# The attention phase of a two-layer network: next rows turned and projected half a slot sooner, their norms' root moved around one mask, and the layernorm chain in three pieces

## The chip, the core and the metric

The kernel runs on one core of one Trainium2 chip. The metric is the device time in microseconds (us). The program has six phases, one after the other, and the change touches the third alone, the linear attention.

Five engines run their own queues in program order and meet at semaphores: TensorE (PE, with its weight loads as PEld), VectorE (DVE), ScalarE (ACT), GpSimd (POOL) and the queues that issue transfers (SP and POOL).

## The reference

Two transformer layers of width 256 on 4 batches of 1024 rows. The attention of the second layer is linear, with positive random features. Cut to what matters here:

```python
qkv = x @ Wqkv + bqkv                                   # 4 x 1024 rows, 16 heads of 16
xn = x / jnp.maximum(jnp.linalg.norm(x, axis=-1, keepdims=True), 1e-12)      # q and k, per head
proj = jnp.einsum('bhtd,rhdm->rbhtm', xn, omega)
feat = jnp.exp(jnp.clip(proj * sqrt_2s - s, -20.0, 20.0)) / np.sqrt(M) ...   # 64 features
# in chunks of 128 rows, with a state carried from chunk to chunk:
kv_cur = jnp.cumsum(kv_prod, axis=2) + kv_state
ctx = jnp.einsum('bhtf,bhtfd->bhtd', q_ch, kv_cur)
out = (ctx / den) @ Wout + bout
x = _layernorm(x + out)
```

## The kernel before, in words

`phase_attention` walks the 1024 rows in eight steps of 128 rows (for all four batches), and each step has eight slots, one for each pair of heads. `body(i)` of every engine writes step i, with the slots t = 0 to 7; bodies -1 and 8 lead in and out. The order on each engine is fixed by this text.

The work of a pair is spread over three slots. In slot t, PE computes the features of pair t (L1192, six matmuls), the scores and turned keys of pair t-1 (L1204, L1210) and the context of pair t-2 (L1224, L1229, L1235). DVE clips the features of pair t (L1380), masks the scores of pair t-1 (L1385) and adds to the state for pair t-2 (L1391). ACT takes the exponentials of pair t (L1270, two), copies the keys of pair t-1 (L1275) and the context of pair t-2 (L1279).

The features have one place in PSUM: PE's features of the next pair wait for DVE's clip of this one. The scores of a pair wait for the mask of the pair before.

Between these stand the projections. A table, `SLOTS_OF_X`, names them by slot and by one of three points: A (after the features), B (after the scores and keys) and C (after the context). The names are: FT, rows of the next step turned; FQ, their q and k projected (FQ 0 to 3, one for each batch); FV, v of this step; FN, normed q and k of the next step turned; BO, context of the step before turned; BC, its quotient turned; BW, its output projection. Each is some matmuls on PE (L1151, L1131, L1162, L1168, L1171) into one of two PSUM banks in turn, and a read by DVE in the same place of its order (`x_evac`); FT, FN and BC are first copied by ACT (`x_high`). A step may start on PE once the step two before it in this order has been read.

Four chains run beside them:

- The norms of the next step's q and k: POOL squares the rows of two batches at a time (L1100) when FQ 1 and FQ 3 have been read; DVE sums (`squares`, L1399), and finds 1/sqrt by a guess (`norm_guess`, L1404 to L1406) and three Newton steps (`norm_newton`, L1409 to L1411), each operation waiting for the one before; POOL multiplies (L1105, in two halves), and PE's FN 0 waits for the first half.
- The layernorm of the step before: DVE's `row_stats` (L1423) when BW has been read, `row_moments` and `row_scales` (L1427 to L1437, the root in L84 to L89), and ACT's `normalise` (L1294).
- The output of BW is written to `z`, which waits until `normalise` of the step before has read it.
- In steps 1 to 6 the weights of the experts are split for a later phase, four chunks a step: ACT rounds a chunk (`expert_high`, L1287, slots 1 to 4), POOL subtracts (L1083), issues a store and a load (L1085, L1087). On POOL, chunks 0 to 2 stand ahead of the two squarings, chunk 3 behind the two multiplications.

Of the kernel before, what the change touches and what calls it, by code (L numbers as in the profile page):

```python
# [9 lines left out]
I32 = mybir.dt.int32  # L10
ALU = mybir.AluOpType
# [4 lines left out]
BATCH, SEQ, D = 4, 1024, 256  # L16
# [63 lines left out]
def rsqrt(chain, v, r, t, ti, ready=None):  # L80


    ve = chain.eng
    chain.link(ve.tensor_scalar(ti, v.bitcast(I32), 1, None, ALU.logical_shift_right))  # L84
    chain.link(ve.tensor_scalar(r.bitcast(I32), ti, -1.0, float(0x5F3759DF), ALU.mult, ALU.add))  # L85
    for n in range(3):
        chain.link(ve.scalar_tensor_tensor(t, r, -0.5, r, ALU.mult, ALU.mult))  # L87
        chain.link(ve.tensor_tensor(t, t, v, ALU.mult))  # L88
        ins = ve.scalar_tensor_tensor(r, t, 1.5, r, ALU.add, ALU.mult)  # L89
        if n == 2 and ready is not None:  # L90
            ins.then_inc(ready, 1)
        else:
            chain.link(ins)
# [810 lines left out]
def phase_attention(nc, x2, bqkv, bout, masks, x3, routed_w, wlo, ids, rows_out, x2_stored, x3_stored, early, x0, x0_in, fc):  # L904

    with ExitStack() as ctx:
# [3 lines left out]
        def sem(name):  # L910
# [52 lines left out]
        A_, B_, C_ = range(3)  # L963
        SLOTS_OF_X = {0: ((B_, "FN", 3), (C_, "BO", 2)),
                      1: ((A_, "BC", 0), (C_, "FV", 0), (C_, "FV", 1)),
                      2: ((A_, "BO", 3), (B_, "FT", 0), (C_, "FT", 1)),
                      3: ((A_, "BC", 1), (B_, "FQ", 0), (C_, "FQ", 1)),
                      4: ((A_, "BW", 0), (B_, "FQ", 2), (C_, "FQ", 3)),
                      5: ((A_, "BW", 1), (C_, "BO", 0)),
                      6: ((A_, "BO", 1), (C_, "FN", 0)),  # L970
                      7: ((A_, "FN", 2), (C_, "FN", 1))}
# [3 lines left out]
        def is_step(n):  # L975
            return not isinstance(n, int) or 0 <= n < STEPS
# [277 lines left out]
        @block.scalar  # L1254
        def _(act):
            act.activation(fc[:, LNA], fc[:, QBIAS], ACT.Ln).then_inc(s["ln_done"], 1)

            def x_high(i, t, point):
                for _, _, name, a, n, h in x_at(i, t, point):
                    if name in HI:  # L1260
                        act.wait_ge(s["x_done"], n + 1)
                        dst = {"FT": xts, "FN": qkt, "BC": ctxt}[name][:, 0, a, :]
                        act.activation(dst, ps[:, x_bank(i, name, a), :], ACT.Copy).then_inc(s["x_hi"], 1)

            def exponentials(n, u):
                act.wait_ge(s["clip_done"], n + 1)

                wait(act, "pair_done", n - 3)
                for q, (dst, bias) in enumerate(((qf, QBIAS), (kf, KBIAS))):
                    act.activation(dst[:, u % 4, :], cf[:, u % 2, q], ACT.Exp, bias=fc[:, bias]).then_inc(s["exp_done"], 1)  # L1270

            def key_rows(n, u):
                act.wait_ge(s["kt_done"], n + 1)
                wait(act, "pair_done", n - 1)
                act.activation(kr[:, u % 2].rearrange("p b f -> p (b f)"), ps[:, KT, :], ACT.Copy).then_inc(s["kr_ready"], 1)  # L1275

            def context_out(i, n, u):
                act.wait_ge(s["pair_done"], n + 1)
                act.activation(ot[:, u], ps[:, OB, 0:2 * P], ACT.Copy).then_inc(s["ot_ready"], 1)  # L1279

            def expert_high(i, c):

                n = (i - 1) * EPER + c
                k = c % 2
                act.wait_ge(eraw_in[k], 16 * ((i - 1) * EPER // 2 + c // 2 + 1))
                act.wait_ge(elo_ready, PRIMED + n)
                act.activation(ehi[:], eraw[:, k], ACT.Copy).then_inc(ehi_ready, 1)  # L1287

            def normalise(i):
                act.wait_ge(s["stats_ready"], i)  # L1290
                act.wait_ge(x2_stored, PRIMED + 16 * STEPS)
                act.wait_ge(s["stored"], PRIMED + 16 * (i - 1))
                for b in range(BATCH):
                    last = act.activation(out[:, b, :], z[:, b, :], ACT.Identity, bias=small[:, 5, b:b + 1], scale=small[:, 3, b:b + 1])  # L1294
                last.then_inc(s["out_ready"], 1)

            def body(i):
                for t in range(PAIRS):
                    if isinstance(i, int) and i == 0 and t == 0:
                        act.wait_ge(s["fc_ready"], 1)  # L1300
                    x_high(i, t, A_)
                    if pair(i, t, 0) is not None:
                        exponentials(*pair(i, t, 0))
                    if pair(i, t, 1) is not None:
                        key_rows(*pair(i, t, 1))
                    x_high(i, t, B_)
                    if pair(i, t, 2) is not None:
                        context_out(i, *pair(i, t, 2))
                    if t == 1 and is_step(i - 2):
                        normalise(i - 1)  # L1310
                    x_high(i, t, C_)
                    if 1 <= t <= EPER and (not isinstance(i, int) or 1 <= i < LAST):
                        expert_high(i, t - 1)
                if isinstance(i, int) and i == STEPS:
                    normalise(i)

            body(-1)
            body(0)
            body(1)
            with act.Fori(2, LAST) as i:  # L1320
                body(i)
            body(LAST)
            body(STEPS)

        @block.vector
        def _(ve):
# [69 lines left out]
            def squares(ch, f, half):  # L1396
                ve.wait_ge(s["sq_ready"], 2 * f + half + 1)
                per = BATCH * HEADS1
                ch.mark(ve.tensor_reduce(nv[:, half * per:(half + 1) * per],  # L1399
                                         sq[:, 2 * half:2 * half + 2].rearrange("p b (n d) -> p (b n) d", d=HD), AX.X, ALU.add))  # L1400
# [7 lines left out]
            def norm_newton(ch, last):  # L1408
                ch.link(ve.scalar_tensor_tensor(nt, nr, -0.5, nr, ALU.mult, ALU.mult))  # L1409
                ch.link(ve.tensor_tensor(nt, nt, nv, ALU.mult))  # L1410
                ins = ve.scalar_tensor_tensor(nr, nt, 1.5, nr, ALU.add, ALU.mult)  # L1411
                if last:
                    ins.then_inc(s["rnorm_ready"], 1)
                else:
                    ch.link(ins)
# [16 lines left out]
                ch.link(ve.tensor_scalar(v, v, 1.0 / D, EPS, ALU.mult, ALU.add))  # L1432
                ch.link(ve.scalar_tensor_tensor(v, half_, 0.25, v, ALU.mult, ALU.add))

            def row_scales(ch):
                rsqrt(ch, v, r, t_, smalli[:])
                ve.tensor_tensor(nb, mean, r, ALU.mult).then_inc(s["stats_ready"], 1)  # L1437
                ch.end()

            def body(i):  # L1440
                norm = Chain(ve, s["norm_own"], NORM_OWN)
                rows = Chain(ve, s["ln_own"], LN_OWN)
                front, back = is_step(i + 1), is_step(i - 1)
                if front:
                    norm.turn(i + 1)
                for t in range(PAIRS):
                    if pair(i, t, 0) is not None:
                        clip(*pair(i, t, 0))
                    x_evac(i, t, A_)
                    if front and t == 6:  # L1450
                        norm_newton(norm, False)
                    if isinstance(i, int) and i == 0 and t == 1:
                        ve.wait_ge(s["weights_in"], WEIGHTS)
                    if pair(i, t, 1) is not None:
                        mask(*pair(i, t, 1))
                    x_evac(i, t, B_)
                    if front and t == 4:
                        squares(norm, i + 1, 0)
                    if front and t == 5:
                        squares(norm, i + 1, 1)  # L1460
                    if front and t == 6:
                        norm_newton(norm, True)
                        norm.end()
                    if pair(i, t, 2) is not None:
                        new_state(*pair(i, t, 2))
                    x_evac(i, t, C_)
                    if front and t == 5:
                        norm_guess(norm)
                        norm_newton(norm, False)
                    if back and t == 6:  # L1470
                        rows.turn(i - 1)
                        row_stats(rows, i)
                    if t == 0 and is_step(i - 2):
                        rows.turn(i - 2)
                        rows.n = BATCH
                        row_moments(rows)
                        row_scales(rows)
                    if isinstance(i, int) and i == STEPS and t == 7:
                        row_moments(rows)
                        row_scales(rows)  # L1480

            body(-1)
            body(0)
# [924 lines left out]
```

## Time and profile before

| | |
|---|---|
| median of 3 runs | 1588.9 us (1588.62 to 1590.71) |
| the profiled execution | 1574.64 us, span 1573.1 us |
| PE busy in the span | 1399.0 us (89%) |
| DVE busy | 920.3 us (59%) |
| ACT busy | 688.8 us (44%) |
| POOL busy | 517.8 us (33%) |
| attention, from its first instruction to its last | about 323 to 848 us of the span |

Busy time is an average over six phases. The rows further down are all of the attention but for three on the clock. A slot is told from the start of its clip (L1380) to the start of the next.

### The profile page before, as it was taken

To read this page: it belongs to the slowest core of one execution; us is meant where nothing else is said; L and a number is where in the kernel's file an instruction comes from. 1 tells how busy PE (TensorE), PEld (TensorE's weight loads), DVE (VectorE), ACT (ScalarE), POOL (GpSimd) and SP (SyncE) were. 2 spreads that over 40 slices of the span, in tenths; PEclk is the share of its full clock that TensorE was granted. 3 is DMA by queue.
4 is the path that set the end of the run, shared out by engine and by line. 5 is a ranking of instruction groups with operands and counts; after the bars stand their busy time and mean duration, and the time that the engine had idled before them with its cause. 6 is when DMAs were issued, how large, how long until landed. Compare 5 with 4: busy or idle time off the path is not lost. (4 is left out here: it accounts for less than half of the span.)

```text
span 1573.1 us, 34052 instructions
## 1 busy us (share of the span) xinstructions
PE 1399.0 (89%) x12248; PEld 1208.8 (77%) x12248; DVE 920.3 (59%) x1994; ACT 688.8 (44%) x1260; POOL 517.8 (33%) x395
## 2 busy tenths in 40 slices
PE   6799999849889889889894899999979999999980
PEld 5688888737667667667673888888879999999980
DVE  4766666656667766777774336443435555555544
ACT  2457656513435435345343323222224555555543
POOL 0245544420343343244300002542203444444440
PEclk7799999959889999999996899999999999999995
DMA  6234321120123133132114601333228888888865
GB/s 250 87 122 149 134 95 63 54 82 15 46 91 110 51 107 123 50 120 93 40 29 152 253 27 61 136 106 116 95 82 224 231 235 242 235 237 230 235 161 220
DMA packets 101209, 204.07 MB, mean 130 GB/s; under 512 B 18448, under 2 KB 72720, under 8 KB 94864
## 3 DMA queue, kind: packets, MB, share of 16 engines
q1 hardware_dynamic: 76032, 144.73, 28.7%
q0 software_dynamic: 23088, 54.31, 12.1%
q10 hardware_dynamic: 2016, 4.08, 0.7%
q8 instruction: 44, 0.72, 0.2%
q14 instruction: 29, 0.24, 0.0%
HBM read 144.53 MB, written 58.55 MB: 129 GB/s over the span
## 5 line engine op out<-in xcount | busy, mean ns | idle before, releaser
L2132 PE MATMUL e_ps<-e_xhl,e_whl 128*128 128x256 f32 x1872 | 248.1, 282 | 5.1 <-DMA e_whl<-wlo 5.1
L2132 PEld LDWEIGHTS e_ps<-e_xhl,e_whl 128*128 128x128 f32 x1872 | 232.9, 189 | 5.6 <-issue 5.6
L1723 PE MATMUL d_ps<-d_xhl,d_whl 128*128 128x512 f32 x768 | 194.8, 403 | 5.3 <-DVE d_whl L1793 5.3
L1723 PEld LDWEIGHTS d_ps<-d_xhl,d_whl 128*128 128x128 f32 x768 | 145.1, 194 | 35.2 <-issue 5.6
L2028 POOL DMA_INDIRECT xs<-e_y,e_slot_id x78 | 121.5, 1558 | 82.8 <-ACT e_y L2059 68.1
L382 POOL TENSOR_TENSOR b_hhl<-b_h,b_hhl 128x512 fp32r<-128x512 f32 x64 | 94.4, 1477 | 138.5 <-ACT b_hhl L609 112.2
L2112 PE MATMUL e_ps<-e_whl,e_ghl 128*128 128x256 f32 x936 | 137.7, 282 | 0.5 <-DVE e_ghl L2206 0.5
L2194 DVE TENSOR_TENSOR e_g<-e_ps,e_act_h 128x256 f32<-128x256 f32 x156 | 66.2, 424 | 116.1 <-ACT e_act_h L2073 115.9
L2112 PEld LDWEIGHTS e_ps<-e_whl,e_ghl 128*128 128x128 f32 x936 | 120.5, 188 | 0.7 <-ACT e_ghl L2083 0.7
L1898 DVE TENSOR_TENSOR d_g<-d_ps,d_act_h 128x512 f32<-128x512 f32 x64 | 44.2, 691 | 127.6 <-PE d_ps L1723 93.9
L475 PE MATMUL b_ps<-b_w,b_hhl 128*128 128x256 f32 x768 | 105.5, 287 | 6.6 <-DVE b_turned_rows L702 5.6
L475 PEld LDWEIGHTS b_ps<-b_w,b_hhl 128*128 128x128 f32 x768 | 99.2, 193 | 12.8 <-issue 6.0
L2073 ACT ACTIVATE e_act_h<-e_ps 128x256 f32<-128x256 f32 x156 | 59.9, 384 | 111.3 <-PE e_ps L2132 111.3
L1270 ACT ACTIVATE c_qf<-c_cf,fc 128x512 f32<-128x512 f32 x64 | 46.3, 723 | 138.9 <-DVE c_cf L1380 138.9
L1702 PEld LDWEIGHTS d_ps<-d_whl,d_ghl 128*128 128x128 f32 x768 | 100.9, 191 | 4.8
L462 PE MATMUL b_ps<-b_xhl,b_w 128*128 128x512 f32 x384 | 104.1, 406 | 0.5 <-ACT b_h L606 0.5
L1702 PE MATMUL d_ps<-d_whl,d_ghl 128*128 128x256 f32 x768 | 104.2, 286 | 0.0
L1083 POOL TENSOR_TENSOR c_elo<-c_eraw,c_ehi 128x1024 fp32r<-128x1024 f32 x24 | 57.0, 2373 | 133.8 <-ACT c_ehi L1287 109.9
L2021 POOL CAST e_whl<-wall 128x1024 fp32r x39 | 40.5, 1039 | 166.1 <-PE e_ps L2112 118.6
L2206 DVE TENSOR_TENSOR e_ghl<-e_g,e_ghl 128x256 fp32r<-128x256 f32 x156 | 66.0, 423 | 41.3 <-ACT e_ghl L2083 41.1
L1380 DVE TENSOR_SCALAR c_cf<-c_ps,fc 128x1024 f32<-128x1024 f32 x64 | 85.7, 1338 | 6.0 <-PE c_ps L1192 4.6
L1769 ACT ACTIVATE d_ghl<-d_g 128x512 fp32r<-128x512 f32 x64 | 40.4, 632 | 103.5 <-DVE d_g L1898 101.3
(304 smaller groups left out, 2686.9 us busy)
## 6 DMA issues: line engine op xcount, KB each, us to landing
e_whl<-wlo SPq DMA_DIRECT2D x39, 1024.0 KB, 5.1
e_whl<-wlo SPq DMA_DIRECT2D x39, 512.0 KB, 3.7
c_eraw<-in_expert_w POOLq DMA_DIRECT2D x24, 512.0 KB, 4.8
wlo<-c_elo POOLq DMA_DIRECT2D x24, 512.0 KB, 3.0
wall<-in_expert_w SPq DMA_DIRECT2D x8, 1536.0 KB, 8.5
xg<-b_zeros POOLq DMA_DIRECT2D x13, 780.0 KB, 3.9
e_xr<-xg SPq DMA_DIRECT2D x39, 260.0 KB, 3.9
x<-rows_out SPq DMA_DIRECT2D x16, 512.0 KB, 3.1
```

The lines of the kernel that those rows point to most:

```text
L382: gp.tensor_tensor(hhl[:, m % 4, 1], h[:, m % 4], hhl[:, m % 4, 0].bitcast(F32), ALU.subtract).then_inc(s["hlo_ready"], 1)
L462: mm = pe.matmul(ps[:, H + m % 2, :], w1s[:, wp, kd, m * P:(m + 1) * P], xhl[:, k, xp, kd, :], start=q == 0, stop=q == 3 * KD - 1)
L475: mm = pe.matmul(ps[:, O + b // 2, lo:lo + D], hhl[:, m % 4, hp, b * P:(b + 1) * P], w2s[:, wp, m, :], start=m == 0 and q == 0 and b % 2 = ...
L1380: ve.tensor_scalar(cf[:, u % 2], ps[:, FB:FB + 2, :], fc[:, HIGH], fc[:, LOW], ALU.min, ALU.max).then_inc(s["clip_done"], 1)
L1702: mm = pe.matmul(ps[:, O + b // 2, (b % 2) * D:(b % 2 + 1) * D], ghl[:, m % 4, gp_, b * P:(b + 1) * P], whl[:, wp_, m // HM, lo:lo + D], s ...
L1723: mm = pe.matmul(ps[:, H + 2 * (m % 2) + w, :], whl[:, wp, e, lo:lo + P], xhl[:, k, xp, kd, :], start=q == 0, stop=q == 3 * KD - 1)
L2028: gp.indirect_dma_start(xs, bass.IndirectOffsetOnAxis(ap=slot_id[:, i, b:b + 1], axis=0), y[:, k, b, :], None, compute_op=ALU.add).then_in ...
L2073: act.activation(act_h[:, m], ps[:, H + m, 0:SLOT], ACT.Silu).then_inc(s["silu_done"], 1)
L2112: mm = pe.matmul(ps[:, O + k, b * D:(b + 1) * D], ghl[:, m, gp_, b * P:(b + 1) * P], whl[:, k, wp_, lo:lo + D], start=m == 0 and q == 0 an ...
L2132: mm = pe.matmul(ps[:, H + m, w * SLOT:(w + 1) * SLOT], whl[:, k, wp, lo:lo + P], xhl[:, k, xp, kd, :], start=q == 0, stop=q == 3 * KD - 1)
L2194: ve.tensor_tensor(g[:, m], ps[:, H + m, SLOT:2 * SLOT], act_h[:, m], ALU.mult).then_inc(s["g_ready"], 1)
L2206: ve.tensor_tensor(ghl[:, m, 1], g[:, m], ghl[:, m, 0].bitcast(F32), ALU.subtract).then_inc(s["glo_ready"], 1)
```

## The change

The table of steps, two lines of it (slots 0, 1 and 5 to 7 stay; in slots 2 to 4 the same steps stand at other points):

```diff
-                      2: ((A_, "BO", 3), (B_, "FT", 0), (C_, "FT", 1)),
-                      3: ((A_, "BC", 1), (B_, "FQ", 0), (C_, "FQ", 1)),
+                      2: ((A_, "FT", 0), (B_, "FT", 1), (C_, "BO", 3)),
+                      3: ((A_, "FQ", 0), (B_, "FQ", 1), (C_, "BC", 1)),
```

ACT's layernorm output goes from the middle of slot 1 to the end of slot 3:

```diff
-                    if t == 1 and is_step(i - 2):
+                    x_high(i, t, C_)
+                    if t == 3 and is_step(i - 2):
                         normalise(i - 1)
-                    x_high(i, t, C_)
```

DVE: the root of the norms is all in slot 5, and the layernorm's chain, which stood whole in slot 0, is now in slots 0, 1 and 3. Its first part, `row_stats`, goes from slot 6 to slot 7.

```diff
+            def row_chain(rows, i, t):
+
+                if t == 0:
+                    rows.turn(i - 2)
+                    rows.n = BATCH
+                    row_moments(rows)
+                if t == 1:
+                    row_guess(rows)
+                    row_newton(rows)
+                if t == 3:
+                    row_newton(rows)
+                    row_newton(rows)
+                    row_shift(rows)
...
                     x_evac(i, t, A_)
-                    if front and t == 6:
+                    if front and t == 5:
+                        squares(norm, i + 1, 1)
+                        norm_guess(norm)
                         norm_newton(norm, False)
...
                         mask(*pair(i, t, 1))
                     x_evac(i, t, B_)
+                    if pair(i, t, 2) is not None:
+                        new_state(*pair(i, t, 2))
+                    if front and t == 5:
+                        norm_newton(norm, False)
+                        norm_newton(norm, True)
+                        norm.end()
+                    x_evac(i, t, C_)
                     if front and t == 4:
                         squares(norm, i + 1, 0)
-                    if front and t == 5:
-                        squares(norm, i + 1, 1)
-                    if front and t == 6:
-                        norm_newton(norm, True)
-                        norm.end()
-                    if pair(i, t, 2) is not None:
-                        new_state(*pair(i, t, 2))
-                    x_evac(i, t, C_)
-                    if front and t == 5:
-                        norm_guess(norm)
-                        norm_newton(norm, False)
-                    if back and t == 6:
+                    if is_step(i - 2):
+                        row_chain(rows, i, t)
+                    if back and t == 7:
```

`row_guess`, `row_newton` and `row_shift` are the two, three and one instructions that `row_scales` held.

DVE's queue in slot 5, before: from the sums of the second two batches (L1399) to the clip of slot 6.

```order
L1399 TENSOR_REDUCE c_nrm<-c_sq 128x64
L1391 TENSOR_TENSOR c_state<-c_ps,c_state 128x128
L1360 TENSOR_SCALAR c_den<-c_ps 128x16
L1361 RECIPROCAL c_den<-c_den 128x16
L1363 TENSOR_TENSOR c_cr<-c_ps,c_den 128x2x4x32
L1404 TENSOR_SCALAR c_nrm<-c_nrm 128x128
L1405 TENSOR_SCALAR c_nrmi<-c_nrm 128x128
L1406 TENSOR_SCALAR c_nrm<-c_nrmi 128x128
L1409 SCALAR_TENSOR_TENSOR c_nrm<-c_nrm 128x128
L1410 TENSOR_TENSOR c_nrm<-c_nrm 128x128
L1411 SCALAR_TENSOR_TENSOR c_nrm<-c_nrm 128x128
L1380 TENSOR_SCALAR c_cf<-c_ps,fc 128x1024
```

DVE's queue in slot 5 of the changed kernel, from the same sums on; L1360, L1361, L1363 and the clip of slot 6 follow behind it.

```order
L1399 TENSOR_REDUCE c_nrm<-c_sq 128x64
L1404 TENSOR_SCALAR c_nrm<-c_nrm 128x128
L1405 TENSOR_SCALAR c_nrmi<-c_nrm 128x128
L1406 TENSOR_SCALAR c_nrm<-c_nrmi 128x128
L1409 SCALAR_TENSOR_TENSOR c_nrm<-c_nrm 128x128
L1410 TENSOR_TENSOR c_nrm<-c_nrm 128x128
L1411 SCALAR_TENSOR_TENSOR c_nrm<-c_nrm 128x128
L1385 TENSOR_TENSOR c_sm<-c_ps,c_tri 128x1024
L1391 TENSOR_TENSOR c_state<-c_ps,c_state 128x128
L1409 SCALAR_TENSOR_TENSOR c_nrm<-c_nrm 128x128
L1410 TENSOR_TENSOR c_nrm<-c_nrm 128x128
L1411 SCALAR_TENSOR_TENSOR c_nrm<-c_nrm 128x128
```

The sums, the guess and the first Newton step now stand ahead of slot 5's mask (L1385), which stood ahead of the sums, and the other two steps, which stood in slot 6 on both sides of its mask, come right behind it.

ACT's queue in slot 3 and at the start of slot 4, before: the quotient's copy (BC 1), the exponentials, the keys, the context copy, and chunk 2 of the experts (L1287).

```order
L1263 ACTIVATE c_ctxt<-c_ps 128x512
L1266 REGISTER_ALU
L1270 ACTIVATE c_qf<-c_cf,fc 128x512
L1270 ACTIVATE c_kf<-c_cf,fc 128x512
L1275 ACTIVATE c_kr<-c_ps 128x512
L1279 ACTIVATE c_ot<-c_ps 128x256
L1285 ISA
L1286 REGISTER_ALU
L1287 ACTIVATE c_ehi<-c_eraw 128x1024
L1266 REGISTER_ALU
L1270 ACTIVATE c_qf<-c_cf,fc 128x512
L1270 ACTIVATE c_kf<-c_cf,fc 128x512
```

The same place in the changed kernel, from slot 3's context copy on.

```order
L1279 ACTIVATE c_ot<-c_ps 128x256
L1261 REGISTER_ALU
L1263 ACTIVATE c_ctxt<-c_ps 128x512
L1292 ISA
L1294 ACTIVATE rows_out<-c_z,c_small 128x256 x4
L1285 ISA
L1286 REGISTER_ALU
L1287 ACTIVATE c_ehi<-c_eraw 128x1024
L1266 REGISTER_ALU
L1270 ACTIVATE c_qf<-c_cf,fc 128x512
L1270 ACTIVATE c_kf<-c_cf,fc 128x512
L1275 ACTIVATE c_kr<-c_ps 128x512
```

BC 1's copy now stands behind the context copy, and the layernorm's output (L1294) with its wait stands between it and chunk 2.

## Rows read from the trace of the kernel before

**Rows 1.** Waits, 330 to 850 us: engine, line, what for, us in total, times, longest.

```profile
PE c_ps L1162 <- POOL c_sq L1105: 46.4, 8, 10.5
```

**Rows 2.** Windows (length; PE, PEld, DVE, ACT, POOL busy; clock; DMA): slot 6, one step.

```profile
576.99:587.88 10.89, 5.73 (x67) 3.65 (x65) 7.01 (x18) 2.68 (x5) 5.69 (x3) 0.79 0.00 0
576.99:638.68 61.69, 56.39 (x714) 42.31 (x713) 44.55 (x89) 27.84 (x48) 23.86 (x17) 0.94 0.28 93
```

**Rows 3.** Timeline: start, duration, what, idle before and its releaser; slot 6.

```profile
582.19 3.82 POOL L1105 TENSOR_TENSOR c_sq<-c_qk,c_nrm 128x1024 f32<-128x1024 f32 x2 [10.95 <-DVE c_nrm L1411]
...
584.17 1.12 PE L1162 MATMUL c_ps<-ident,c_sq 128*128 128x128 f32 x4 [5.16 <-POOL c_sq L1105]
```

**Rows 4.** Timeline of PE: the features that open slots 0, 1, 2, 4, 5 and 6.

```profile
592.82 0.97 PE L1192 MATMUL c_ps<-c_qkt,early 32*128 32x512 f32 x6
...
598.15 0.97 PE L1192 MATMUL c_ps<-c_qkt,early 32*128 32x512 f32 x6
...
606.48 0.96 PE L1192 MATMUL c_ps<-c_qkt,early 32*128 32x512 f32 x6
...
620.29 0.96 PE L1192 MATMUL c_ps<-c_qkt,early 32*128 32x512 f32 x6
...
629.22 0.97 PE L1192 MATMUL c_ps<-c_qkt,early 32*128 32x512 f32 x6
...
635.74 0.50 PE L1192 MATMUL c_ps<-c_qkt,early 32*128 32x512 f32 x2
```

**Rows 5.** Timelines of ACT (slot 1), POOL and DVE (slot 4), same step.

```profile
606.24 2.07 ACT L1294 ACTIVATE rows_out<-c_z,c_small 128x256 f32<-128x256 f32 x4
608.20 1.05 ACT L1287 ACTIVATE c_ehi<-c_eraw 128x1024 fp32r<-128x1024 f32 x1
...
622.60 2.37 POOL L1083 TENSOR_TENSOR c_elo<-c_eraw,c_ehi 128x1024 fp32r<-128x1024 f32 x1 [1.88 <-DMA wlo<-c_elo]
...
626.79 1.91 POOL L1100 TENSOR_TENSOR c_sq<-c_qk 128x1024 f32<-128x1024 f32 x1
...
628.73 1.22 DVE L1399 TENSOR_REDUCE c_nrm<-c_sq 128x64 f32<-128x1024 f32 x1 [2.05 <-POOL c_sq L1100]
```

**Rows 6.** Timeline of DVE: row statistics, slot 5's pieces.

```profile
586.56 1.39 DVE L1423 BATCH_NORM_STATS2 c_stats<-c_z 128x6 f32<-128x256 f32 x4
...
631.92 0.68 DVE L1372 TENSOR_TENSOR c_z<-c_ps,c_xb 128x512 f32<-128x512 f32 x1
632.95 1.22 DVE L1385 TENSOR_TENSOR c_sm<-c_ps,c_tri 128x1024 f32<-128x1024 f32 x1 [0.35 <-PE c_ps L1204]
...
635.91 0.16 DVE L1360 TENSOR_SCALAR c_den<-c_ps 128x16 f32<-128x16 f32 x1
...
636.74 0.22 DVE L1404 TENSOR_SCALAR c_nrm<-c_nrm 128x128 f32<-128x128 f32 x1
...
637.51 0.29 DVE L1409 SCALAR_TENSOR_TENSOR c_nrm<-c_nrm 128x128 f32<-128x128 f32 x1
```

**Rows 7.** Timeline of DVE, slot 0: clip, FN 3's read, first and last of the scales.

```profile
594.19 1.34 DVE L1380 TENSOR_SCALAR c_cf<-c_ps,fc 128x1024 f32<-128x1024 f32 x1
...
597.98 0.69 DVE L1342 TENSOR_TENSOR c_qkt<-c_ps,c_qkt 128x512 fp32r<-128x512 f32 x1 [1.32 <-ACT c_qkt L1263]
...
600.49 0.17 DVE L84 TENSOR_SCALAR c_smalli<-c_small 128x4 int32<-128x4 int32 x1
...
602.67 0.16 DVE L1437 TENSOR_TENSOR c_small<-c_small 128x4 f32<-128x4 f32 x1
```

**Rows 8.** PE after two other waits, in the timeline, and windows with the clock.

```profile
42.03 0.41 PE L403 MATMUL b_ps<-ident,b_bt 128*128 128x128 f32 x2 [1.73 <-ACT b_ct L568]
44.00:46.00 2.00, 2.00 (x11) 2.00 (x11) 1.67 (x10) 0.00 (x0) 0.00 (x0) 0.50 0.00 0
1189.13 1.07 PE L2132 MATMUL e_ps<-e_xhl,e_whl 128*128 128x256 f32 x7 [2.44 <-DMA e_whl<-wlo]
1190.00:1192.00 2.00, 2.00 (x19) 2.00 (x18) 0.76 (x2) 0.69 (x2) 0.00 (x0) 1.00 1.10 443
```

More of the change, by code:

```diff
@@ L965, in phase_attention @@
                       1: ((A_, "BC", 0), (C_, "FV", 0), (C_, "FV", 1)),
-                      2: ((A_, "BO", 3), (B_, "FT", 0), (C_, "FT", 1)),
-                      3: ((A_, "BC", 1), (B_, "FQ", 0), (C_, "FQ", 1)),
-                      4: ((A_, "BW", 0), (B_, "FQ", 2), (C_, "FQ", 3)),
+                      2: ((A_, "FT", 0), (B_, "FT", 1), (C_, "BO", 3)),
+                      3: ((A_, "FQ", 0), (B_, "FQ", 1), (C_, "BC", 1)),
+                      4: ((A_, "FQ", 2), (B_, "FQ", 3), (C_, "BW", 0)),
                       5: ((A_, "BW", 1), (C_, "BO", 0)),
@@ L1433, in row_moments, with row_guess, row_newton, row_shift @@
                 ch.link(ve.scalar_tensor_tensor(v, half_, 0.25, v, ALU.mult, ALU.add))
-            def row_scales(ch):
-                rsqrt(ch, v, r, t_, smalli[:])
+            def row_guess(ch):
+                ch.link(ve.tensor_scalar(smalli[:], v.bitcast(I32), 1, None, ALU.logical_shift_right))
+                ch.link(ve.tensor_scalar(r.bitcast(I32), smalli[:], -1.0, float(0x5F3759DF), ALU.mult, ALU.add))
+            def row_newton(ch):
+                ch.link(ve.scalar_tensor_tensor(t_, r, -0.5, r, ALU.mult, ALU.mult))
+                ch.link(ve.tensor_tensor(t_, t_, v, ALU.mult))
+                ch.link(ve.scalar_tensor_tensor(r, t_, 1.5, r, ALU.add, ALU.mult))
+            def row_shift(ch):
                 ve.tensor_tensor(nb, mean, r, ALU.mult).then_inc(s["stats_ready"], 1)
                 ch.end()
+            def row_chain(rows, i, t):
[10 more added lines that the diff above has]
+                    row_shift(rows)
             def body(i):
@@ L1456, in body @@
                     x_evac(i, t, B_)
+                    if pair(i, t, 2) is not None:
[5 more added lines that the diff above has]
+                    x_evac(i, t, C_)
                     if front and t == 4:
                         squares(norm, i + 1, 0)
-                    if front and t == 5:
-                        squares(norm, i + 1, 1)
-                    if front and t == 6:
-                        norm_newton(norm, True)
-                        norm.end()
-                    if pair(i, t, 2) is not None:
-                        new_state(*pair(i, t, 2))
-                    x_evac(i, t, C_)
-                    if front and t == 5:
-                        norm_guess(norm)
-                        norm_newton(norm, False)
-                    if back and t == 6:
+                    if is_step(i - 2):
+                        row_chain(rows, i, t)
+                    if back and t == 7:
                         rows.turn(i - 1)
                         row_stats(rows, i)
[L1473 to L1480, printed above, removed]
+                        if isinstance(i, int) and i == STEPS:
+                            row_moments(rows)
+                            row_guess(rows)
+                            row_newton(rows)
+                            row_newton(rows)
+                            row_newton(rows)
+                            row_shift(rows)
             body(-1)
```

## The prediction

> **What bounds the kernel now.** I read the waits of the attention first, then the windows by slot, then the timelines of one step. PE is busy for most of a step, and the waits show one long stall: PE waits for POOL's normed rows eight times, 46.4 us in all, 10.5 of it in the lead-in [rows 1]. That leaves 35.9 us in seven steps, 5.1 each (0 to 6; step 7 has no next rows). The timeline shows it: FN 0 in slot 6 starts after 5.16 us of idle PE, 1.98 us after POOL's multiplication, which itself followed DVE's last Newton step [rows 3].
>
> A step lasts 61.7 us, and its slot 6 alone 10.9 at a mean clock of 0.79 [rows 2]. PE's own need at full clock comes from the starts of its features. Slot 0, with two turns, takes 5.33 us; slot 1, 8.33; slots 2 and 3 together 13.81; slot 4, 8.93; slot 5, 6.52 [rows 4]. Slots 6 and 7 also have two turns each, so 5.33 each. The sum is 53.6 us. So of 61.7 us, 5.2 is the stall and, by difference, 2.9 is PE at 1.2 in place of 2.4 GHz behind it. Together 8.1 us a step can be won at most, if nothing else comes late.
>
> **The change, part by part.** The table moves steps within slots 2, 3 and 4 only, so PE's slot lengths stay. I follow one step of the new order from p2 = 0, the start of PE's features in slot 2, round to the next p2. T is the start of a clip.
>
> 1. To slot 4's features: 13.8 [rows 4]. BC 1 is now last in slot 3. Its copy by ACT and DVE's read end about 1.4 us behind it (0.1, 0.6, and 0.68 as for a read of this size, rows 6). Then DVE does the third piece of the layernorm chain, two Newton steps and the shift. The whole guess, three steps and shift took 2.18 us from first to last start, eleven instructions of 0.2 [rows 7], so seven take 1.4. T4 = 13.8 + 1.4 + 1.4 = 16.6. Before, the clip followed PE's features by about 1.1.
> 2. ACT's `normalise` waits for that chain. What is queued behind it on ACT is chunk 2 of the experts and slot 4's exponentials. Four activations take 2.07 and the chunk 1.05 [rows 5], with 0.2 of hand-over: POOL starts chunk 2 at 16.6 + 3.3 = 19.9. Behind chunk 2 on POOL stand two DMA issues and the squares of batches 0 and 1, 4.19 us later (622.60 to 626.79), and DVE's sums start 1.94 after that (628.73) [rows 5]. So DVE starts the sums at 26.0 and T5 = 27.2, where PE's features alone would allow 13.8 + 8.9 + 1.1 = 23.8 and DVE's own queue 24.8. This hand-back, about 2.4 us a step, is what the move of `normalise` costs. Before, chunk 2 was held by its store's landing instead (1.88 us, rows 5).
> 3. Slot 5 on DVE: clip 1.26 (its 1.34 less the overlap of the next start), BW 1's read 0.68, sums 1.2, guess 0.77 (636.74 to 637.51), Newton step 1.17 with the wait for its end (638.68, the end of the step's window, less 637.51), mask 1.14, state 0.2, two steps of 0.98, BO's quotient 0.83 [rows 2, 5, 6, 7]. The sum is 9.2, so T6 = 36.4. The mask ends at 33.6.
> 4. PE reaches slot 6's scores at 13.8 + 8.9 + 6.5 + 1.5 = 30.7. They wait for that mask, which is now late: a hole of 2.9 us. The root is ready at 35.6, and 2.0 later [rows 3] FN 0 can start, at 37.6. PE gets there at 33.6 + 3.4 = 37.0 (5.33 less the features' 0.9 and two turns of about 0.5), so the old stall is now 0.6.
> 5. Slot 6 on DVE: as in slot 0, clip to the read of a normed step is 3.79 (594.19 to 597.98, rows 7): ACT's two exponentials and key copy stand ahead. With the context copy ahead too (0.2) and 0.6 for the read, T7 = 41.0. Slot 7: 4.0 + 0.6 and now the row statistics, 1.39 [rows 6]: T0 = 47.0.
> 6. PE's BC 0 in slot 1 needs FN 3 read: 47.0 + 3.79 + 0.69 = 51.5. PE gets there at 49.8, a hole of 1.7. From BC 0 to the next p2 is 8.33 less 0.9 for the features, 7.4. The step closes at 58.9.
>
> Check: 53.6 + 2.9 + 0.6 + 1.7 = 58.8. Slot 0's clip-to-clip falls by the 2.2 us of the chain that left it, and slot 1 takes 1.0 of them, under PE's 8.33 us slot.
>
> So steps 2 to 6 gain 61.7 - 58.8 = 2.9 us each, 14.5 in all. Steps 0 and 1 have no layernorm chain, and step 0 no chunks. T5 then follows PE (T4 waits for PE, not for a chain), the mask and FN 0 are in time, and of 8.1 us only the 1.7 before BC 0 comes back: about 6.5 each, 13. Lead-in, step 7 and lead-out I take at nothing: in the lead-in the same chain runs with one sum less ahead of FQ 3's read (up to 1.2 us gained, the length of a sum, rows 5); in step 7 PE sets the pace and the new piece in slot 3 lies under PE's slot 4; in the lead-out the scales leave the path of BO 3 (up to 2.2 gained, rows 7) but `normalise` may hold up the last BW (up to 2.1 lost, rows 5). Bounds for the three: -3 to +2.
>
> Sum: 14.5 + 13 = 27.5 us, against the profiled execution's 1574.6 (span 1573.1). It stands 14.3 us below the median of the runs; I take the difference over unchanged: 1588.9 - 27.5 = 1561.4, say 1561.
>
> SP's queue keeps its order. The store behind `normalise` and the load of the rows behind it go out two slots later, and FT needs them half a step later still. `z` is read by `normalise` at the start of slot 4 and written at its end, 6 us later.
>
> **A rule weighed.** After 1.73 us of wait at 42 us, on a thinly used PE, the clock stood at 0.50 two us later; after 2.44 us at 1189, with dense work before and behind, it stayed at 1.00 [rows 8]. The holes of 2.9 and 0.6 have dense work between them, so I take 1.00 as likelier. The Trainium skill ("TensorE: Matmul & The Clock Gate", A second HAM failure mode: psum-queue depth-cycling) says that frequent short idles between groups of matmuls make the clock swing between its two levels. By that rule the time would be the first rival's, and the rows do not exclude it.
>
> **The rivals.** A, the clock falls in the new holes of steps 2 to 6. A fall costs PE 2.9 us as now; the hole before BC 0 can hide up to 1.7 of it. That is 1.2 to 2.9 a step, 6 to 14.5 in all: 1567 to 1576. For it speaks the row at 42 us, against it that at 1189.
>
> B, chunk 2 does not hold up the sums, because DVE's chain or ACT is quicker than I put it. Then T5 is 2.4 us earlier, and PE's hole goes with it: 5 x 2.4 = 12 us more, 1549. For it speaks only that the links are short; against it that each stands in one queue.
>
> C, part of the stall comes back elsewhere, in waits between PE and DVE in slots 7, 0 and 1 that the walk misses, say 2 us a step in seven: 1575. DVE is busy 44.6 of 61.7 us [rows 2], so in a step of 58.8 it has 14 us free, and slots 5 to 0 hold little of it.
>
> D, slower: chunk 2 comes later still, behind the landing of chunk 1's store as well as behind `normalise`. Each us it is late goes one for one through the sums, the mask and the scores of slot 6. From 2.3 us late the hole there is as long as the old stall (5.2), the clock falls as it does now, and the gain of steps 2 to 6 is 2.9 - 2.3 - 2.9 = -2.3 each. The 13 us of steps 0 and 1 still cover this; from 2.6 us late they no longer do, and 3.7 us late gives 5 x 3.7 - 13 = 5.5 us slower, 1594. Before, that landing held chunk 2 by 1.88 us, with the chunk's copy long done [rows 5]; now the copy comes 5 us later in the slot, which speaks against it.
>
> E, no change: `normalise` and the stall trade places exactly. It needs a loss of 5.5 us in each of the five steps with no fall of the clock, and nothing points there.
>
> **How the numbers follow.** The forecast (1553 to 1567) 0.50, A 0.18, B 0.13, C 0.09, D 0.06, E 0.04. The likeliest gives 1561. From B's 1549 with the bounds of the lead-in and lead-out to A's and C's upper end the range is 1546 to 1577, which leaves out D, E and a little of C. Faster by over 0.2% (3.2 us, about what a measurement can tell from no change) are the forecast, A, B and C, 0.90; E is 0.04 and D 0.06.
>
> **What the profile would show.** The wait of PE's FN (L1162) for POOL's L1105 falls from 46.4 us to about 15, 10 of it the lead-in. Scores (L1204) of slot 6 wait for the mask (L1385), nearly 3 us in steps 2 to 6 and not in 0 and 1. POOL's chunk 2 is released by ACT's L1287, no longer by the DMA. Clip to clip, slots 4 and 5 are about 10.6 and 9.2, slot 6 is 4.6, slot 0 near 6.3; a middle step is 58.8. The clock over it is 1.00. I am wrong if chunk 2 starts before 18 (B) or after 22 (D) behind slot 2's features, if the clock over a step is under 0.97 (A), or if steps 0 and 1 are longer than 57.

## The result, and the profile after

The changed kernel takes 1566.8 us (median of 4 runs, 1563.5 to 1571.4) beside 1588.8 for the kernel before on the same chip: ratio 0.9861, 95% interval 0.983 to 0.9892, 22.0 us. Its profiled execution took 1569.4, span 1567.8. The forecast was 1561, its range 1546 to 1577.

First the waits of the attention, 330 to 850 us, to set beside [rows 1].

```profile
POOL c_elo L1083 <- ACT c_ehi L1287: 157.5, 18, 16.7
...
ACT rows_out L1294 <- DVE c_small L1445: 22.0, 8, 7.2
...
PE c_ps L1162 <- POOL c_sq L1105: 11.3, 4, 9.8
PE c_ps L1204 <- DVE c_sm L1385: 10.5, 6, 2.0
PE c_ps L1171 <- DVE c_qkt L1342: 6.0, 6, 1.3
```

The old stall fell from 46.4 to 11.3 us, 9.8 of it in the lead-in. In its place the scores wait for the mask, six times: in steps 2 to 6, as forecast, and for 1.06 us in step 0, where none was forecast.

The windows by slot of step 4 (slots 4 to 7, then the step), to set beside [rows 2]:

```profile
612.14:622.70 10.56, 10.56 (x130) 8.49 (x128) 5.79 (x8) 6.07 (x10) 6.57 (x5) 1.00 0.58 184
622.70:631.55 8.85, 6.39 (x82) 4.69 (x80) 8.37 (x22) 2.09 (x4) 1.34 (x2) 0.87 0.25 76
631.55:636.13 4.58, 4.58 (x67) 3.25 (x68) 4.11 (x8) 2.71 (x6) 4.58 (x3) 0.88 0.00 0
636.13:642.55 6.42, 6.42 (x100) 5.00 (x99) 5.28 (x11) 3.27 (x6) 4.43 (x4) 1.00 0.49 163
583.45:642.55 59.10, 55.23 (x714) 41.70 (x713) 45.33 (x91) 27.28 (x48) 23.89 (x17) 0.97 0.30 98
```

Slot 6 has gone from 10.9 to 4.6 us, slot 4 takes 10.6, and the step 59.1. Step 3 of the same execution (slots 5 to 7, then the step) is 3 us longer:

```profile
560.63:569.49 8.86, 6.40 (x90) 4.62 (x90) 8.38 (x22) 2.09 (x4) 1.35 (x2) 0.91 0.25 77
569.49:574.92 5.43, 5.43 (x55) 3.45 (x54) 4.20 (x8) 2.69 (x5) 5.43 (x3) 0.50 0.00 0
574.92:583.45 8.53, 8.53 (x104) 6.67 (x104) 5.47 (x9) 3.40 (x6) 3.55 (x4) 0.81 0.38 123
521.39:583.45 62.06, 58.20 (x714) 43.48 (x713) 45.62 (x90) 27.38 (x48) 23.86 (x17) 0.92 0.29 93
```

Slots 0 to 5 agree within 0.02 us with those of step 4, but slots 6 and 7 run at a clock of 0.50 and 0.81 and last 3.0 us longer. The timeline of step 4 shows the walk: the features of slot 2 (its origin), the layernorm's output and chunk 2 on ACT, chunk 2 and the squares on POOL, the first sums and slot 5's mask on DVE. PE has two larger holes in it, 1.99 us at slot 6's scores (L1204) and 0.89 before BC 0 (L1171). The rows stand by engine.

```profile
595.01 0.97 PE L1192 MATMUL c_ps<-c_qkt,early 32*128 32x512 f32 x6
...
626.30 0.63 PE L1168 MATMUL c_ps<-ident,c_ot 128*128 128x128 f32 x4 [0.47 <-ACT c_ot L1279]
628.92 1.35 PE L1204 MATMUL c_ps<-c_qf,c_kf 64*128 64x128 f32 x12 [1.99 <-DVE c_sm L1385]
...
647.07 0.66 PE L1171 MATMUL c_ps<-ident,c_cr 128*128 128x128 f32 x4 [0.89 <-DVE c_qkt L1342]
...
612.23 2.08 ACT L1294 ACTIVATE rows_out<-c_z,c_small 128x256 f32<-128x256 f32 x4 [2.11 <-DVE c_small L1445]
614.21 1.04 ACT L1287 ACTIVATE c_ehi<-c_eraw 128x1024 fp32r<-128x1024 f32 x1
...
615.42 2.37 POOL L1083 TENSOR_TENSOR c_elo<-c_eraw,c_ehi 128x1024 fp32r<-128x1024 f32 x1 [8.22 <-ACT c_ehi L1287]
...
619.62 3.75 POOL L1100 TENSOR_TENSOR c_sq<-c_qk 128x1024 f32<-128x1024 f32 x2
...
621.56 1.22 DVE L1399 TENSOR_REDUCE c_nrm<-c_sq 128x64 f32<-128x1024 f32 x1 [2.41 <-POOL c_sq L1100]
...
627.55 1.22 DVE L1385 TENSOR_TENSOR c_sm<-c_ps,c_tri 128x1024 f32<-128x1024 f32 x1
```

And the clock behind the hole, in windows of 2 us (PE busy, clock, DMA): step 4 first, then step 3.

```profile
627.00:629.00 2.00, 0.08 (x2) 1.00 0.49 174
629.00:631.00 2.00, 2.00 (x18) 0.57 0.00 0
631.00:633.00 2.00, 2.00 (x32) 0.58 0.00 0
633.00:635.00 2.00, 2.00 (x38) 1.00 0.00 0
...
567.00:569.00 2.00, 2.00 (x20) 0.71 0.00 0
569.00:571.00 2.00, 2.00 (x33) 0.50 0.00 0
...
577.00:579.00 2.00, 2.00 (x28) 0.73 0.89 260
```

After the same hole of 1.99 us TensorE ran at 1.2 GHz for under 4 us in step 4 and for about 10 in step 3.

### The profile page after: what moved, and what is told of

It reads as the page before. It is cut to its first block and busy times, and to the rows that moved or that the text cites. A ratio compares the mean times of both kernels' runs of the same rounds, so it can differ in the third digit from the quotient of the medians.

```text
span 1567.8 us, 34049 instructions
## 1 busy us (share of the span) xinstructions
PE 1402.0 (89%) x12248; PEld 1210.3 (77%) x12248; DVE 923.0 (59%) x1994; ACT 686.0 (44%) x1260; POOL 517.0 (33%) x395
## 5 line engine op out<-in xcount | busy, mean ns | idle before, releaser
L1723 PE MATMUL d_ps<-d_whl,d_ghl 128*128 128x256 f32 x768 | 108.2, 290 | 6.6 <-issue 6.2
L1723 PEld LDWEIGHTS d_ps<-d_whl,d_ghl 128*128 128x128 f32 x768 | 103.5, 195 | 12.5 <-issue 7.9
L1204 PE MATMUL c_ps<-c_qf,c_kf 64*128 64x128 f32 x1024 | 81.0, 301 | 11.6 <-DVE c_sm L1385 10.5
L1204 PEld LDWEIGHTS c_ps<-c_qf,c_kf 64*128 64x128 f32 x1024 | 68.1, 202 | 28.5 <-issue 25.8
```

The lines of the kernel that those rows point to most:

```text
L1204: mm = pe.matmul(ps[:, SC + h, cols], kf[f, u % 4, cols], qf[f, u % 4, cols], start=True, stop=True)
L1723: mm = pe.matmul(ps[:, O + b // 2, (b % 2) * D:(b % 2 + 1) * D], ghl[:, m % 4, gp_, b * P:(b + 1) * P], whl[:, wp_, m // HM, lo:lo + D], s ...
```

## The experiments

Step lengths are from clip to clip of slot 0, in us, read from the timeline of VectorE (L1380). All ratios are to the kernel before, timed on the same chip.

### The three parts alone

The root alone (`squares`, guess and steps in slot 5, as the change writes them; the table and the layernorm chain as before):

```diff
-                    if front and t == 6:
+                    if front and t == 5:
+                        squares(norm, i + 1, 1)
+                        norm_guess(norm)
                         norm_newton(norm, False)
...
```

> The kernel before with the root of the norms alone moved: sums of the second half, guess and first Newton step ahead of slot 5's mask, the other two behind it. Table of steps and layernorm chain as before. My theory (the stall at FN 0 is the cost, and what the full change gives back comes from the layernorm's output ahead of chunk 2): the stall goes, nothing new is ahead of chunk 2, so a middle step is about 56.5 us (61.7 before) and the whole is 1548 to 1554, that is faster than the full change. Rival (the gain needs the projections half a slot sooner, since FQ 3 is read only at the end of slot 4 and POOL's squares then hold DVE in slot 5): a stall of 2 to 3 us stays and the whole is about 1575.

The table alone (its three lines for slots 2 to 4; the third puts FQ 2 and FQ 3 at A and B of slot 4, BW 0 at C):

> The kernel before with the table of steps alone changed (FT and FQ at points A and B, BO 3, BC 1 and BW 0 at C of slots 2 to 4). My theory: the root still ends in slot 6, so the stall of 5.2 us with the slow clock behind it stays in all seven steps: 1586 to 1592. Rival (sooner projections are what frees the norms): at least a third of the gain, 1581 or less.

The layernorm chain alone (`row_chain`, `row_stats` in slot 7, `normalise` in slot 3):

> The kernel before with the layernorm chain alone changed (moments in slot 0, guess and one step in slot 1, two steps in slot 3, output on ACT at the end of slot 3, row statistics in slot 7). My theory: slot 0 is 2.2 us shorter on DVE where PE has slack anyway, and the output stands ahead of chunk 2, so the sums of slot 4 come 1.5 to 2.4 us later in steps 2 to 6 and the stall with them: 7 to 12 us slower, 1596 to 1601. Rival (the whole chain in slot 0 was a bound of its own): 5 to 10 us faster.

| before: 1591.4 | time, us | ratio (95% interval) | steps 2 to 6 |
|---|---|---|---|
| root alone | 1548.9 | 0.9722 (0.9707 to 0.9737) | 55.8 to 56.5 |
| table alone | 1587.5 | 0.998 (0.9965 to 0.9996) | 61.5 to 61.9 |
| layernorm chain alone | 1604.6 | 1.0079 (1.0064 to 1.0094) | 64.3 to 65.5 |

The root is the whole gain, and alone gains twice what the change does: PE's wait for the normed rows, 5.0 to 5.2 us a step before, is 0.6 us at most in steps 0 to 6. The table is worth 0 to 0.35%. The third part costs 13 us, a little more than expected. Its stall at FN 0 is 6.6 us in steps 2 to 5, for 5.2 before. Windows of its step 3 (slots 6 and 7, then the step):

```profile
584.44:594.49 10.05, 3.43 (x28) 2.08 (x28) 5.78 (x14) 2.68 (x5) 4.84 (x3) 0.65 0.00 0
594.49:603.01 8.52, 8.52 (x104) 6.66 (x104) 5.47 (x9) 3.40 (x6) 4.83 (x4) 0.81 0.37 123
537.95:603.01 65.06, 56.41 (x714) 42.31 (x713) 45.27 (x90) 27.19 (x48) 23.95 (x17) 0.92 0.27 89
```

POOL's squares come 1.8 us later behind slot 2's clip than before, and slot 7 now runs at 0.81, 8.5 us long for 6.3 before.

### What the third part costs inside the change

The change without it, that is, root and table together:

> The change without its layernorm-chain part: before, with the root drawn together in slot 5 and with the table that turns and projects the next rows half a slot sooner and turns the normed rows from slot 6 on. Theory (the table is worth nothing by itself, the third part costs): a step of about 56.3 us like the kernel with the root alone (1548.9), total 1545 to 1551. Rival (the earlier table pays once the root no longer bounds): a step under 55.5 us, 1542 or less.

It took 1543.9 us, ratio 0.971 (0.9696 to 0.9724), a little under the expected 1545 to 1551. Steps 2 to 6 were all 55.8, with the clock at 1.00 in each of their slots. Its step 3:

```profile
514.08:569.87 55.79, 54.05 (x715) 40.50 (x713) 44.58 (x91) 27.25 (x48) 23.94 (x17) 1.00 0.32 104
```

So with the others present the third part costs 23 us by the times and 24 by the ratios (0.9861 to 0.971). Its interval overlaps that of the root alone, so nothing speaks for the rival, that the table pays more then: the step fell by 0.6 us only.

Next, the hand-back through ACT. In the changed kernel, chunk 2 is evicted ahead of `normalise`:

```diff
-                    if t == 3 and is_step(i - 2):
-                        normalise(i - 1)
                     if 1 <= t <= EPER and (...):
                         expert_high(i, t - 1)
+                    if t == 3 and is_step(i - 2):
+                        normalise(i - 1)
```

> The full change, but in slot 3 ACT rounds chunk 2 first and writes the layernorm's output after it. My theory: the sums of slot 4 no longer wait for POOL's chunk 2 behind the output, slot 4 falls from 10.6 to about 8.2 us, the hole at slot 6's scores (2.0 to 2.9 us) closes, and with it most falls of the clock: steps 2 to 6 about 56.4 us, the whole 1550 to 1556 (1567 for the full change). Rival (DVE's own queue in slots 4 and 5 sets the pace): within 3 us of the full change.

1547.8 us, 0.9719 (0.9705 to 0.9732), below the expected 1550 to 1556. In steps 2 to 6 PE's wait for the mask at slot 6's scores is gone and the clock is 1.00 in slots 5 to 7. Steps 2 to 5 are 56.2 to 57.2, step 6 is 58.6. The clock still falls elsewhere: in slots 0 and 1 of steps 2 and 4, and in slot 4 of step 6 (0.74). One edit of order gives back nearly all of it, 19 us by the times and 23 by the ratios. Slot 4 fell from 10.6 to 6.1, but slot 3 grew from 8.8 to 10.9, which I had not expected. The timeline of POOL and DVE there:

```profile
543.95 2.36 POOL L1083 TENSOR_TENSOR c_elo<-c_eraw,c_ehi 128x1024 fp32r<-128x1024 f32 x1 [4.02 <-ACT c_ehi L1287]
...
543.48 0.15 DVE L1440 SCALAR_TENSOR_TENSOR c_small<-c_small 128x4 f32<-128x4 f32 x1
...
544.06 2.27 DVE L1440 SCALAR_TENSOR_TENSOR c_small<-c_small 128x4 f32<-128x4 f32 x1
```

A VectorE operation on 4 elements a partition, 0.15 us otherwise, lasts 2.27 and ends within 0.02 us of POOL's pass on chunk 2. It is so in each of steps 2 to 6; in step 6 the chain's last operation (L1445) lasts 2.39 us as well, to the end of a squaring on POOL, and slot 3 takes 13.0. To test it, the same kernel with slot 3's piece of the chain (two Newton steps and the shift) ahead of the read at point C, so that it is done before the pass starts:

```diff
+                    if t == 3 and is_step(i - 2):
+                        row_chain(rows, i, t)
                     x_evac(i, t, C_)
...
-                    if is_step(i - 2):
+                    if t != 3 and is_step(i - 2):
                         row_chain(rows, i, t)
```

> The changed kernel with chunk 0 evicted before the normalise in slot 3 (which gave 1547.8, with VectorE's small subtraction of the shift lasting 2.27 us instead of 0.16, until the end of GpSimd's pass beside it), and besides with the two Newton steps and the shift of slot 3 issued before GpSimd's pass on chunk 2 can have started. Theory (the small operation is held by GpSimd's pass, not by its own operands): it lasts 0.16 us again, slot 3 falls from 10.9 to about 8.8 us, the step by 1 to 2, total 1543 to 1548. Rival (the operation is slow for a reason of its own or other small operations are held instead): some 2 us operation stays in the chain and the total stays within 1546 to 1552.

(The chunk moved in slot 3 is chunk 2, and the long operation is the first of a Newton step, L1440.)

```profile
542.85 2.38 POOL L1083 TENSOR_TENSOR c_elo<-c_eraw,c_ehi 128x1024 fp32r<-128x1024 f32 x1 [4.02 <-ACT c_ehi L1287]
...
541.78 0.16 DVE L1440 SCALAR_TENSOR_TENSOR c_small<-c_small 128x4 f32<-128x4 f32 x1
...
542.38 0.16 DVE L1445 TENSOR_TENSOR c_small<-c_small 128x4 f32<-128x4 f32 x1
```

The long operation is gone and slot 3 takes 8.2 to 8.7 us. But slot 4 takes most of it back, 8.5 to 8.7 for 6.1, and steps 2 to 5 are 56.1 to 57.0. The total, 1546.9 (0.9738, 0.9716 to 0.976), is not told apart from that of the kernel it was made from (1547.8, 0.9719). PE is by now busy for 53.8 of the 56.1 us of step 3, and its longest wait is 1.28 us before BC 0.

### One hole or two

By the prediction's walk the hole at the scores and the small one at FN 0 both come of the lateness of the root's chain. Here the first group of the root stands behind slot 5's mask:

```diff
-                    if front and t == 5:
-                        squares(norm, i + 1, 1)
-                        norm_guess(norm)
-                        norm_newton(norm, False)
...
                         mask(*pair(i, t, 1))
+                    if front and t == 5:
+                        squares(norm, i + 1, 1)
+                        norm_guess(norm)
+                        norm_newton(norm, False)
```

> The changed kernel with one edit: in slot 5 the sums, the guess and the first Newton step of the root stand behind the mask instead of ahead of it. Theory (the two holes of a step are one debt, the lateness of the root, paid in two places): the mask of slot 6 is then on time, the hole of 2.9 us at the scores of slot 6 goes, the root is ready at the same moment and the hole at slot 6's expand chunk 0 grows from 0.6 to about 3.5 us; a step at full clock stays at 58.8 us, the total between 1560 and 1572. Rival (the order around the mask is what saves or costs time): without the hole at the scores the step falls by 2 us or more, 1550 or less; or the root comes later by the mask's two passes, about 2 us a step, 1578 or more.

1564.9 us, 0.9846 (0.9828 to 0.9864), no different from the change. The wait for the mask is gone, and PE's wait at slot 6's FN 0 is back, 1.95 us (not 3.5) in each of steps 2 to 6. Its windows of slots 5 to 7 in step 5 (in step 2 alone the clock did not fall behind it):

```profile
679.80:688.65 8.85, 7.24 (x130) 5.17 (x128) 8.37 (x21) 2.09 (x4) 1.34 (x2) 1.00 0.24 80
688.65:693.24 4.59, 3.27 (x17) 2.08 (x18) 4.12 (x8) 2.85 (x6) 4.59 (x3) 0.75 0.00 0
693.24:701.70 8.46, 8.46 (x100) 6.56 (x99) 5.27 (x10) 3.24 (x6) 4.38 (x4) 0.73 0.35 124
```

Slots 5 and 6 have the lengths of step 4 of the change to 0.01 us, and the clock falls behind the new place of the hole. The order around the mask moves the hole and saves nothing.

### What is left of the step

Root as in the change, and in slot 1 chunk 0 evicted ahead of `normalise`:

> The kernel before with the root drawn together in slot 5, and besides in slot 1 ScalarE evicts expand chunk 0 before it normalises. Theory: with the root gone the step of 56.3 us is a circle of ScalarE's eviction of chunk 0 and GpSimd's chunks; with chunk 0 released some 2.1 us sooner the step falls to about 54.5, total 1538 to 1545. Rival (TensorE's own work of 53.6 and its other waits bound the step, and the circle is not closed by chunk 0): the step stays at 56 to 56.5, total 1546 to 1551.

And both additions together:

> The kernel before with the root drawn together, the earlier table, and chunk 0 evicted ahead of the normalise in slot 1: both edits that took the step from 56.4 to 55.8 us when added alone to the root. Theory (at 55.8 us the step is TensorE's own work with gaps that neither edit touches): a step of 55.8 again, 1541 to 1546. Rival (each edit still hides a wait that the other shows): a step of 55.3 us or less, 1541 or less.

1544.4 us (0.9717, 0.9702 to 0.9732) with steps of 55.8, and 1546.3 (0.9717, 0.9704 to 0.973) with steps of 55.8 to 56.5. The first total is within its forecast and the second 0.3 us above, but the step of 54.5 expected of the first did not come: either addition takes 0.6 us off the root's 56.4, both together no more. With root and table PE is busy 54.1 of 55.8 us (above), so little is left. Three short waits of PE for reads by DVE make up 1.6 us of the other 1.7 in its step 3 (0.65, 0.47 and 0.46); none of them was tried. No version beat the change without its third part (1543.9), and none of these differs from another by more than the intervals.

### The same kernels once more

> The kernel before, profiled once more. Its first profiled execution took 1574.6 us beside 1588 to 1591 in all others, and its shared-expert phase (first matmul of the shared weights to the first of the expert phase) took 316.5 us, where the profiles of the changed kernels show 330 to 334 with a pause of TensorE in it. Theory (the first profile lacked a pause that most executions have): about 1587 to 1591 us, the shared phase about 330 us with the pause, the attention steps 61 to 62 us as before. Rival (the change to the attention made the shared phase longer): the shared phase again 316 to 317 us.

> The changed kernel, profiled once more. In the first profile the granted clock fell to between 0.5 and 0.9 in slots 5 to 7 of steps 2 to 5, behind the hole at the scores of slot 6, and its steps took 64.6, 62.1, 59.1 and 60.3 us. Theory (the hole makes the clock fall, how far depends on the moment): falls in the same slots again, of other depths, steps between 58.8 and 65, sum of steps 2 to 5 between 240 and 250 us. Rival (the falls belong to that one execution): clock 1.00 in all slots and every step 58.8 us.

The kernel before took 1589.2 us, and its shared-expert phase (first matmul L1723 to first L2132) 329.8 us, where the first profile had 316.6. Windows of PE, the first profile's and then the second's:

```profile
982.00:1002.00 20.00, 20.00 (x117) 1.00 0.50 173
```

```profile
982.00:1002.00 20.00, 14.26 (x66) 0.97 0.28 100
1002.00:1022.00 20.00, 18.11 (x91) 0.86 0.23 87
```

The changed kernel has the pause in both its profiles (phase 330.3 and 330.4 us). So it is no effect of the change. The first profile of before was the exception: of the 14.6 us between the two executions, 13.2 lie in this phase, and that is nearly all of the 14.3 by which it stood under the median.

The changed kernel took 1563.9 us. Steps 2 to 6, first profile: 64.6, 62.1, 59.1, 60.3, 57.5; second: 60.2, 60.1, 59.1, 60.2, 57.5. The clock fell in slots 5 to 7 of each of steps 2 to 5 in both, behind the same hole, and to different depths. Steps 2 to 5 sum to 246.0 and 239.7 us, the second just under the expected 240. The two executions differ by 5.5 us, and the start of the shared phase by as much (841.77 and 836.28). The second step 3, slots 5 and 6 of which had clocks of 0.79 and 0.71 (0.91 and 0.50 in the first), lasted 1.9 us less.

## Why the prediction came out right, and where it was off

**The base and the sum.** 27.5 us were forecast. From one profile to the other, the start of the shared phase came 19.3 us sooner (861.05 to 841.77), and between the second profiles 26.2 (862.45 to 836.28). The medians differ by 22.0. Step by step it is a sum of misses both ways. Steps 2 to 6, the largest term, were to gain 14.5 us; they gained 4.8 from first profile to first and 11.3 from second to second. Steps 0 and 1 gained 13.2 and 14.0 for 13, the ends 1.3 and 0.9 for nothing. To carry the difference over to the median was right: the missing 14 us of the profile lay outside the attention.

**The walk.** From the features of slot 2 in step 4 (595.01), forecast and measured:

| | forecast | measured |
|---|---|---|
| T4 | 16.6 | 17.1 |
| POOL starts chunk 2 | 19.9 | 20.4 |
| sums start | 26.0 | 26.6 |
| T5 | 27.2 | 27.7 |
| PE at slot 6's scores | 30.7 | 31.9 |
| hole there | 2.9 | 2.0 |
| mask ends | 33.6 | 33.8 |
| root ready | 35.6 | 35.8 |
| T6, T7, T0 | 36.4, 41.0, 47.0 | 36.5, 41.1, 47.5 |
| hole before BC 0 | 1.7 | 0.9 |
| step | 58.8 | 59.1 |

Step (1) missed 0.5 us, and PE waited 0.52 us for turned rows in slot 3 on the way; the times up to T5 keep that distance, and slot 5 on DVE took less than the sum made it (8.85 for 9.2; its own terms also put the mask's end at 33.4, not 33.6). Steps (4) and (6) put PE too early at both places, since they left out PE's short waits (0.52 and 0.47 us), and before BC 0 the slow clock besides. So the holes were 2.0 and 0.9. The hole of 0.6 at FN 0 did not come in steps 2 to 5; in step 6, at full clock, it was 0.47. Step (2), the hand-back of `normalise` through chunk 2, was right in mechanism: evicting the chunk first took the hole away. Its price was set too low: 2.4 us a step, 12 in all, was the time on the chain. Measured, undoing it is worth 19 to 23 us and the whole part 23 to 24, since the hole also brings a clock fall, and the step without it is nearly all PE's own work (53.8 of 56.2 us in step 3).

**Steps 0 and 1.** 6.5 us each were forecast; 6.9 and 6.3 came in the first profiles, 7.5 and 6.5 in the second. Step 6, forecast like 2 to 5, took 57.5. Its hole was 1.49 us and the clock stayed at 1.00. Lead-in, step 7 and lead-out gave 1.3 us, within the bounds of -3 to +2.

**The clock: rival A was there.** The step of the prediction that failed is the weighed rule. I held 1.00 likelier, because the hole had dense work on both sides like the row at 1189. It fell behind eight of eight holes of 1.99 us (two profiles, steps 2 to 5), and not behind step 6's of 1.49 and 1.51. By the prediction's own sign, a step's clock under 0.97, A is what happened in six of these eight steps. The row at 42 us was also less unlike the holes than "thinly used" says: in the trace of before PE is busy for all of 32 to 40 us ahead of that wait. With slots 6 and 7 of the kernel without the hole (4.59 and 5.90) as measure, the falls cost 4.8, 3.5, 0.5 and 1.7 us in the first profile, 10.5 in all, inside A's 6 to 14.5, and 4.2 in the second, below it. Step 2 has another fall behind its 1.28 us before BC 0 (0.90 and 0.87 in slots 0 and 1). The 1566.8 measured is nearer to A's 1567 than to the forecast's 1561. That the forecast was so near is in part luck: how deep the clock falls changed from execution to execution, and step 6 was 1.3 us shorter than forecast. The Trainium skill ("TensorE: Matmul & The Clock Gate", A second HAM failure mode: psum-queue depth-cycling) says that PE's frequent short idles between groups of matmuls make the clock swing. The trace agrees so far that the clock fell behind a hole of 1.99 us with dense work around it, which my reading of the row at 1189 spoke against; the 2.44 us there and step 6's 1.49 without a fall show that the length of a hole alone does not tell. Removing the hole (evicting chunk 2 first) removed the fall behind it, and moving it moved the fall, so the link is shown. Why the clock came back after under 4 us in one step and 10 in another stays open.

**B, C, D, E.** Chunk 2 did hold the sums (B fell); no wait of 2 us a step arose elsewhere in slots 7, 0 and 1 (C fell); chunk 2 was released by ACT, 0.5 us after the forecast, never by the store's landing (D fell). What of the shown-by list was wrong is the clock (0.87 to 0.97 in steps 2 to 5), the mask's hole (2.0 for "nearly 3") and a hole of 1.06 at the scores in step 0.

## What to carry to other kernels

When one change bundles a cure with rearrangements, time the parts alone: here one part was worth over 40 us, one next to nothing, and one cost 13 alone and 23 beside the others. On an in-order queue ask of every moved instruction what stands behind it for another engine; swapping two neighbours on ScalarE gave back 19 us or more. And price a hole in TensorE's work with a possible clock fall behind it, dense work around it or not.

## What the runs showed of the hardware

**A small VectorE operation held by GpSimd.** L1440, which reads two SBUF tensors of 4 elements a partition, lasts 0.15 to 0.16 us, and 2.27 when it starts 0.1 us into GpSimd's 2.36 us pass (so in four of four steps; 2.22 in a fifth, where it starts 0.2 us in). The Trainium skill ("SBUF — State Buffer", SBUF: two separate sides) says that the port pair shared by the two engines is an exclusive lock held for a whole instruction, and names VectorE operations with two SBUF inputs among those that take it. The trace agrees, and moving the operation out of the pass brought 0.16 us back. L1436, a shift with one SBUF input, is held as well, until 0.03 us after the pass ends; POOL and DVE in slot 1 of the changed kernel:

```profile
594.52 2.38 POOL L1083 TENSOR_TENSOR c_elo<-c_eraw,c_ehi 128x1024 fp32r<-128x1024 f32 x1 [15.35 <-ACT c_ehi L1287]
...
595.73 1.20 DVE L1436 TENSOR_SCALAR c_smalli<-c_small 128x4 int32<-128x4 int32 x1
```

**The same hole, with and without a fall.** In the kernel with chunk 2 first and the steps sooner, PE waits 1.27 to 1.28 us before BC 0 in each of steps 2 to 6. The clock fell behind it in steps 2, 4 and 6 (0.91, 0.88 and 0.85 over slot 0) and stayed at 1.00 in 3 and 5. Likewise a wait of 1.49 us was followed by a fall in the kernel with chunk 2 first (step 6, slot 4, 0.74) and by none in the change (step 6, slot 5). That the clock held in one step does not show that such a hole is free.

**A pause in a phase that nothing touched.** In the second profile of before and the first of the change, PE issues matmuls one or a few at a time, with gaps of 0.2 to 2.2 us, for some 15 us of the shared-expert phase, with "issue" as the only releaser. The gaps sum to 7 to 8 us, behind them the clock is at 0.50 for 7 us in the one and 10 in the other, and the phase is 13 to 14 us longer than without. It is that long, 328.8 to 333.5 us, in twelve of the thirteen profiled executions, and 316.6 in the first of before. The cause was not tried.
